# A step's shift passes through the ring of maximum banks seven units behind the step's last unit instead of four

## What is computed

```
x = x + 0.5 * ffn(layernorm(x), W_fc, W_proj)
x = x + attention(layernorm(x))      # 16 heads of 16, rotary q and k, causal, softmax
x = x + 0.5 * ffn(layernorm(x), W_fc, W_proj)
```

## Time and profile before

| | |
|---|---|
| median of 3 runs | 1463.99 us (1461.68 to 1468.61) |
| profiled execution, its own time | 1472.26 us |
| its span | 1470.5 us |
| TensorE (PE) busy | 1321.8 us, 90% |
| VectorE (DVE) busy | 1130.7 us, 77% |
| ScalarE (ACT) busy | 860.0 us, 58% |
| GpSimd (POOL) busy | 223.1 us, 15% |
| mean granted TensorE clock | 0.944 |

### The profile page before, as it was taken

How to read it: one execution, slowest core, us unless ns; L and a number is a source line. 1 busy time by engine, 2 the same in 40 slices (tenths; PEclk the granted TensorE clock), 3 DMA queues, 4 the chain that set the end, 5 groups by cost and what they waited for, 6 DMA issues and landing times. The chain is left out here.

```text
span 1470.5 us, 22187 instructions
## 1 busy us (share of the span) xinstructions
PE 1321.8 (90%) x8224; PEld 793.6 (54%) x8224; DVE 1130.7 (77%) x2638; ACT 860.0 (58%) x1157; POOL 223.1 (15%) x205
## 2 busy tenths in 40 slices
PE   4988888976799999999999999999999989999996
PEld 3877777854543343443444343443443435888886
DVE  6567767697688897898888888888988952676665
ACT  4644545511066675676666666666766777555554
POOL 4002222232210110110110110210201021001000
PEclk9999999986689998999999999999999989999999
DMA  3114433682173070160430520700701121243212
GB/s 114 44 65 136 136 134 104 143 238 94 46 121 58 14 112 9 30 96 9 63 63 9 94 33 9 111 15 9 125 9 35 48 72 59 78 135 125 87 44 72
DMA packets 88740, 110.30 MB, mean 75 GB/s; under 512 B 25308, under 2 KB 60892, under 8 KB 87004
## 3 DMA queue, kind: packets, MB, share of 16 engines
q1 hardware_dynamic: 88632, 108.88, 31.5%
HBM read 64.62 MB, written 42.21 MB: 73 GB/s over the span
## 5 line engine op out<-in xcount | busy, mean ns | idle before, releaser
L989 ACT ACTIVATE probs<-s_ps 128x1024 f32<-128x1024 f32 (+3 forms) x640 | 541.8, 896 | 263.1 <-PE s_ps L1094 261.7
L1010 DVE TENSOR_REDUCE maxes<-m_ps 128x1 f32<-128x512 f32 x768 | 489.3, 684 | 70.5 <-PE m_ps L1073 68.5
L1073 PE MATMUL m_ps<-kT,qT 64*128 64x512 f32 (+3 forms) x1280 | 447.0, 457 | 57.9 <-DVE maxes L1010 39.6
L1073 PEld LDWEIGHTS m_ps<-kT,qT 64*128 64x128 f32 x1280 | 201.5, 192 | 411.9 <-DVE maxes L1010 278.3
L1094 PE MATMUL s_ps<-qT,kT 64*128 64x512 f32 (+3 forms) x1280 | 316.1, 402 | 7.0 <-ACT probs L989 6.8
L1110 PE MATMUL o_ps<-probs,v_w 128*32 128x512 f32 (+3 forms) x2560 | 311.7, 560 | 0.2 <-POOL probs L958 0.2
L1013 DVE CUSTOM_DVE_ANT_0 masked<-m_ps,mask 128x384 f32<-128x384 f32 (+3 forms) x512 | 233.6, 485 | 54.2 <-PE m_ps L1073 52.2
L1094 PEld LDWEIGHTS s_ps<-qT,kT 64*128 64x128 f32 x1280 | 171.4, 192 | 37.1 <-ACT probs L989 30.7
L958 POOL TENSOR_SCALAR_AFFINE_SELECT probs<-probs 128x512 f32<-128x512 f32 x128 | 82.2, 642 | 717.8 <-ACT probs L989 717.8
L508 DVE TENSOR_TENSOR h_lo_c<-hsq_c,h_hi_c 128x512 fp32r<-128x512 f32 x64 | 46.6, 728 | 79.2 <-ACT h_hi_c L339 40.9
L330 ACT ACTIVATE relu_a<-ups_a 128x512 f32<-128x512 f32 x64 | 38.1, 596 | 101.8 <-PE ups_a L605 100.8
(11 more groups left out here) (124 smaller groups left out, 1879.3 us busy)
## 6 DMA issues: line engine op xcount, KB each, us to landing
qT<-qkT_parts SPq DMA_DIRECT2D x96, 128.0 KB
kT<-qkT_parts SPq DMA_DIRECT2D x48, 256.0 KB
qkT_parts<-qk_hi_a SPq DMA_DIRECT2D x32, 256.0 KB, 5.1
qkT_parts<-qk_lo_a SPq DMA_DIRECT2D x32, 256.0 KB, 4.8
sumsT<-osum SPq DMA_DIRECT2D x32, 256.0 KB, 2.6
table_a<-in_rot SPq DMA_DIRECT2D x8, 768.0 KB, 7.5
xin_a<-in_x SPq DMA_DIRECT2D x8, 512.0 KB, 3.6
xres_a<-in_x SPq DMA_DIRECT2D x8, 512.0 KB, 5.1
```

Of the source, the lines that this page charges most:

```text
L989: act.activation(probs[:, b % PBUF, 2 * hp:2 * hp + 2, off:CH], s_ps[hp][:, :, off:CH], ACT.Exp, scale=D ** -0.5).then_inc(exp_done, 1)
L1010: dve.tensor_reduce(out, m_ps[:, i % MB, 0:width], AX.X, ALU.max).then_inc(max_read, 1)
L1073: pe.matmul(m_ps[:, i % MB, 0:width], qT[n % 2][r0:r0 + HR, j, hp, t * P:(t + 1) * P], kT[n % 2][r0:r0 + HR, hp, k * CH:k * CH + width], s ...
```

## The change

`ring_order` inserts each shift behind the fourth unit that follows the step's last unit in the order. The number becomes seven, `3 + MB + 1`. Nothing else is edited; the places of all units stay, the item numbers behind a moved shift change with it.

```
+BEHIND_LAST = 3 + MB + 1
...
-            after = [i for i, (_, e) in enumerate(order) if i > last and e[0] == "unit"][:4]
+            after = [i for i, (_, e) in enumerate(order) if i > last and e[0] == "unit"][:BEHIND_LAST]
             at = after[-1] if after else last
             order.insert(at + 1, (order[at][0], ("shift", n, j)))
```

## The result

The changed kernel takes 1474.87 us (median of 14 runs, 1469.31 to 1482.55), the kernel before 1466.24 (14 runs, 1461.68 to 1473.58): ratio 1.0064, interval 1.0048 to 1.0080. It is slower by 8.6 us. The forecast was +2.1 us; the measured time lies 0.9 us above the upper end of the range. The range stood on a median of 3 runs of the kernel before, 1463.99 us; over 14 runs that kernel is 2.3 us slower, so by how little the range was missed says nothing. The difference was four times the forecast.

A forecast was written before the change was run, and what follows sets the result against it. It took TensorE's in-order queue, tied to VectorE by the ring, as the bound. Steps 0, 1, 2, 3 and the phase ahead gave 0.5 + 3.0 + 0 - 0.6 - 0.8 = +2.1 us on 1463.99: 1466.1, range 1456 to 1474.

The forecast's parts named there:

- step 0: Slots 24 to 26 of a group: transpose's wait goes but u9 falls behind the products; net +0.07 us, bounds -0.42 to +0.26.
- step 2: Slots 4 to 6: some items come 0.6 us earlier, later units wait for the same reads; net 0, bounds -0.42 to +0.27.
- the signs: Observations named to show it right or wrong, such as `negparts` waits 9.0 to about 1.6 us, slot 24's products 0.5 earlier.
- Step 3: Slot 20: the shift's transpose no longer stands ahead of the products; -0.08 us a group, bounds -0.15 to +0.28.
- the phase ahead: The two shifts ahead of the attention: units with banks free sooner take their places; -0.8 us together, between -2.3 and 0.
- The copy of step 3: The shift's copy in slot 20, now behind u7 on VectorE, was to come 1.9 us later.
- step 1's products: Slots 31 to 33: products start 0.18 us earlier, u9 falls behind them, next products later; net +0.43, bounds 0 to +0.54.
- the clock: Half-clock stretches near steps 3 and 0 change in number: about 15 us won (chance 0.07), or 1481 us (chance 0.06).
- The wait is won: TensorE's waits at the shifts and behind them go without being given back: 13.8 us won, 1450.2 us; chance 0.13.
- The shift of step 3 lands too late: Slot 24's scores wait for the shift's DMAs; up to 1.9 us seven times, +13.3, 1477.3 us; chance 0.06.
- Step 0 loses as step 1: Slots 24 to 26 lose 0.43 us more seven times, plus 0.27 per step 2 and 3 copy: +9.2, 1473.2 us; chance 0.06.

The follow-up runs named there:

- S between the halves: Against the kernel before: only step 1's shift at seven units, slot 32 cut so its units keep their pieces and the transpose stands between the score halves; 1469.58 us, ratio 1.0018.
- the four sets: Four series of experiment kernels, each measured beside the kernel before on the same chip; that kernel's medians were 1465.0 to 1469.7 us over 98 runs.
- the third set: Series with the changed kernel measured again beside the kernel before (1465.13 us) on the same chip; the changed kernel took 1475.15 us, ratio 1.0063.
- slot 32 recut: Against the kernel before: shifts stay at four units, only slot 32 is cut 1, 0, 1, 2 as in the changed kernel; 1471.08 us, ratio 1.0034.
- Step 1 at nine: Against the kernel before: step 1's shift nine units behind the last one, behind slot 32's products, all other shifts at four; 1465.06 us, ratio 0.9999.
- cut by units alone: Against the kernel before: all shifts at seven units, slots cut by their units only, so a shift no longer moves the borders; 1468.86 us, ratio 1.0030.

## Why the prediction was wrong

**What was right.** The four kinds of shift were the right unit of account, and two of the four came out as worked: step 0 +0.07 (forecast +0.07), step 2 +0.02 (0). In step 0 the products of slot 25 (named slot 24 among the signs) came 4.58 us behind slot 24's first scores instead of 5.11, the 0.53 that was worked out. Step 3 gained -0.24, more than its -0.08 and past its bound of -0.15. For the phase ahead the -0.8 has a -0.9 beside it that other kernels show to be no measure. The waits moved as forecast, `negparts` 9.0 to 1.6. In step 0 u5's bank set S (0.27 idle) and u12 waited 0.67. The copy of step 3 came 1.8 us later in its slot (forecast 1.9).

**The step that failed: step 1's products.** "S takes the place of u8 and u8 that of u9, so the products start at 699.40 instead of 699.58." u7 did start earlier, 2.90 us after slot 31's first scores as worked out, but the products started 1.53 behind it and not 1.11: +0.42. I had counted items, one for one, and not which of them start together. The sign of it was in the trace of the kernel before: S has 128*32 where units have 64*128, and u8 in that place (698.81) started at the same time as a score matmul. Measured alone, S between the halves costs 0.40 a group, the cut 0.38 (forecast 0.43 with the products 0.18 earlier); 7 x 0.40 = 2.8 us was missing from the sum. In the whole miss of 6.5 us (8.6 less 2.1) the order accounts for some 1.8, since step 3 gave 1.1 back; the rest, 4.7, is the next point. My bound for step 1, 0 to +0.54, took only the delays of units and did not hold 0.84.

**The rival that came in on top: the clock.** I gave a loss by the clock 0.06, "the small waits change place, hardly their sum". The sum of the forecast has no term for it. Another number of stretches at half clock was named as a sign of being wrong, and the traces have eleven where they had nine. By the trace the sum of the waits did grow, 25 us more for `maxes` against 7.4 less for `negparts`. In the comparison 4.7 us are left for the clock (8.6 measured less 3.9 of the order; 3.8 if the order's part is the 4.8 without slot 0); that is a remainder, for the clocks of the kernel before are on record only in the four sets. Measured in the third set it is 6.4 by the slope. It was less than the +15 of the rival, which had as many new stretches as there were old ones. The Trainium skill (TensorE: Matmul & The Clock Gate, the section on psum-queue depth-cycling) has the clock swing with small idle times between matmul groups; this agrees with a loss here in sign (the waits for banks grew, the mean clock fell), but not with place: slot 5 falls in one group and not in the next, and also with nothing changed near it.

**The other rivals.** *The wait is won:* no, `maxes` took over the wait. *The shift of step 3 lands too late:* in the group 883 to 986 the copy ended at 980.15 and slot 24's first scores stood at 985.57, 5.4 us, and slots 23 and 24 did not stretch: hidden, with 5.4 of the former 7.4 left from the copy's end; from the fourth DMA's issue some 3.4 are left, against a forecast of 3.5. No run shows the landing itself. The 2 us that the prediction takes from the Trainium skill (DMA: Bandwidth & Descriptors, Anatomy of one DMA) are fitted there to transfers that GpSimd issues; these are issued by SP. *Step 0 loses as step 1:* no, +0.07.

**What stays open.** What decides in which group the clock falls. With slot 32 recut, 0.38 us a group, the mean fell by 0.0025 (0.9493 against 0.9518); with S between the halves, 0.40 us a group, it did not (0.9502 against 0.9498), so the length of the group alone does not set it. Step 1 at nine, with the shift moved further but the group's length kept, kept it (0.9509 against 0.9498); cut by units alone, it fell by 0.0046. That the mean clock goes with the order rather than with the chip rests on one set for each kernel except the changed one, which has two. Also open: why the starts on either side of S are 0.11 longer each, and whether its 128 rows are the reason.

## What to carry to other kernels

Before an item is put between two others, see in the timeline which matmuls start at the same time: between half-height ones an item over all rows of the array cost 0.59 us here, its own start and longer ones beside it, while right behind the products it cost 0.18. When a kernel derives a cut from a count (here the quarters of a slot), a moved item changes the cut too; price it as a second change, since here it was half of the loss. And hold each run's mean clock beside its time: two profiled executions of equal span can come from kernels 0.6% apart.

## What the hardware showed unexpectedly

A transpose of 0.28 us costs 0.40 to 0.42 us more between the score halves than behind the products (step 1 at nine: +0.04). TensorE's mean clock went with the order of a group in ways that the slots around it do not show: a reorder worth 2.7 us cost 5.9 where the mean clock went from 0.9518 to 0.9493, and the full change 10.0 where its slots make 3.9 to 4.8, at 0.9459. One thousandth of the mean clock is 1.08 us of this kernel.
